# Attention one: where the products for the row maxima stand among the scores

## What is computed

```python
h = h + _L0_attn_ref(_layernorm(h, axis=-1), Wqkv, bqkv, Wr, br)

def _L0_attn_ref(x, Wqkv, bqkv, Wr, br):          # b 8, c 1024, h 16, he 16
    xh = x.reshape(b, c, h, he).transpose(0, 2, 1, 3)
    q, k, v = jnp.split(jnp.einsum('bhce,ef->bhcf', xh, Wqkv) + bqkv, 3, axis=-1)
    att = jnp.einsum('bhqe,bhke->bhqk', q, k) / jnp.sqrt(jnp.float32(he))
    mask = jnp.tril(jnp.ones((c, c), dtype=att.dtype), k=-1)
    att = jax.nn.softmax(att * mask, axis=-1)
    out = jnp.einsum('bhqk,bhke->bhqe', att, v)
    return out.transpose(0, 2, 1, 3).reshape(b, c, d) @ Wr + br
```

## Time and profile before

| | |
|---|---|
| median of three runs | 2999.05 us (2997.51 to 3005.18) |
| profiled execution | 3005.22 us, its span 3002.8 us |
| first attention | about the first 1500 us of the span, 14 loop iterations of two windows in it |
| mean granted TensorE clock | 0.928 of full speed |

### The profile page before, as it was taken

How to read it: one execution, slowest core, us unless ns; L and a number is a source line. 1 busy time by engine, 2 the same in 40 slices (tenths; PEclk the granted TensorE clock), 3 DMA queues, 4 the chain that set the end, 5 groups by cost and what they waited for, 6 DMA issues and landing times. The chain is left out here.

```text
span 3002.8 us, 58475 instructions
## 1 busy us (share of the span) xinstructions
PE 2581.3 (86%) x15254; PEld 1510.3 (50%) x15318; DVE 2118.6 (71%) x5668; ACT 1523.5 (51%) x3246; POOL 1640.4 (55%) x2564
## 2 busy tenths in 40 slices
PE   1778988888988888888868999898998979999999
PEld 0323433333333333343345666666666647666666
DVE  2657766777766767676567999898888965556554
ACT  1345555555555655555513655555555634444444
POOL 3664343333334333334245877777776757777675
PEclk7679999999999999999969999999999979999999
DMA  3353343344343344334230000000000000000000
GB/s 56 89 116 62 52 63 54 52 70 69 51 63 56 53 59 70 58 54 63 36 137 1 1 1 1 1 1 1 1 1 1 1 3 16 16 14 16 16 16 18
DMA packets 81300, 113.27 MB, mean 38 GB/s; under 512 B 25100, under 2 KB 37144, under 8 KB 80536
## 3 DMA queue, kind: packets, MB, share of 16 engines
q1 hardware_dynamic: 76360, 101.44, 19.8%
q0 software_dynamic: 3072, 8.39, 1.0%
q10 hardware_dynamic: 1744, 2.16, 0.2%
HBM read 18.98 MB, written 8.39 MB: 9 GB/s over the span
## 5 line engine op out<-in xcount | busy, mean ns | idle before, releaser
L554 ACT ACTIVATE probs<-scoresT 128x512 f32<-128x512 f32 x1152 | 639.7, 604 | 632.4 <-PE scoresT L697 622.9
L643 DVE TENSOR_REDUCE cand<-ring 128x4 f32<-128x512 f32 x1152 | 724.1, 680 | 219.6 <-PE ring L753 167.3
L476 POOL TENSOR_SCALAR_AFFINE_SELECT probs<-probs 128x256 f32<-128x256 f32 x512 | 204.9, 414 | 468.5 <-ACT probs L554 462.4
L697 PE MATMUL scoresT<-stage 98*128 98x512 bf16 (+3 forms) x1536 | 410.3, 344 | 22.2 <-ACT probs L554 16.6
L753 PE MATMUL ring<-Km,Qm 64*128 64x512 bf16 (+2 forms) x1792 | 253.0, 321 | 160.5 <-DVE cand L643 130.5
L717 PE MATMUL pv<-probs,Vg 128*32 128x512 f32 (+3 forms) x3072 | 325.2, 545 | 28.3 <-POOL probs L476 25.9
L753 PEld LDWEIGHTS ring<-Km,Qm 64*128 64x128 bf16 x1792 | 83.5, 95 | 375.6 <-DVE cand L643 239.5
L1180 PE MATMUL mm<-w_W,hT 128*128 128x256 f32 x1024 | 259.1, 399 | 8.7 <-ACT z L1268 2.8
L1200 PE MATMUL mm<-w_W,x2T 128*128 128x512 f32 x512 | 242.4, 596 | 0.3 <-DVE x L1419 0.2
L697 PEld LDWEIGHTS scoresT<-stage 98*128 98x128 bf16 x1536 | 114.5, 99 | 234.4 <-issue 139.1
L1261 ACT ACTIVATE hT<-mmT,w_be,w_g 128x128 f32<-128x128 f32 x512 | 185.5, 469 | 90.7 <-PE mmT L1191 90.7
(11 more groups left out here) (254 smaller groups left out, 5280.9 us busy)
## 6 DMA issues: line engine op xcount, KB each, us to landing
stage<-parts SPq DMA_DIRECT2D x256, 96.0 KB, 2.8
stage<-parts SPq DMA_DIRECT2D x256, 64.0 KB, 2.8
Qm<-parts SPq DMA_DIRECT2D x128, 128.0 KB, 2.6
Km<-parts SPq DMA_DIRECT2D x128, 128.0 KB, 2.7
stage<-parts SPq DMA_DIRECT2D x256, 32.0 KB, 2.4
out<-result SPq DMA_DIRECT2D x64, 128.0 KB, 1.7
stage<-ct SPq DMA_DIRECT2D x128, 4.0 KB
w_W<-in_W SPq DMA_DIRECT2D x4, 512.0 KB
```

The costliest lines, as they stand in the source:

```text
L476: nc.gpsimd.affine_select(out=d, in_=d, compare_op=ALU.is_gt, fill=0.0, base=0, pattern=[[0, 2], [1, P]], channel_multiplier=-1).then_inc( ...
L554: nc.scalar.activation(probs[:, buffer(slot), :], scoresT[slot % SCORE_BANKS][:], ACT.Exp, scale=SOFT).then_inc(exp_ok, 1)
L643: ins = nc.vector.tensor_reduce(c, src[:].rearrange("p (t a b) -> p t a b", t=c.shape[1], b=P), AX.X, ALU.max)
L697: ins = nc.tensor.matmul(scoresT[slot % SCORE_BANKS][:, at:at + hi - lo], Ks[0:ROWS, gi, hh, P * kt:P * kt + P], Qs[0:ROWS, gi, hh, lo:hi] ...
```

## The change

The units of the maxima are put two at a time (four banks, the whole ring) at nine positions `MAX_AT`, the same in both windows, instead of one at a time at 18. Bursts 0 to 3 move from 9, 12, 20, 28 to 11, 15, 22, 30, so that with bursts 4 and 5 (at 0 and 3, unmoved) six of the nine groups have a burst at their position. `PV_HALF`, the copy of the first half of `pv`, moves from 14 to 17, behind burst 1. In the prologue without scores (`ALONE`) the units stand one position apart.

```diff
-BURST_AT = {0: 9, 1: 12, 2: 20, 3: 28}
+BURST_AT = {0: 11, 1: 15, 2: 22, 3: 30}
+
+MAX_AT = (0, 3, 7, 11, 15, 18, 22, 26, 30)
...
-    0: {... "MX": 2, "MX_END": 32, "MX_CURVE": 1.0, "PV_HALF": 14},
-    1: {... "MX": 1, "MX_END": 32, "MX_CURVE": 1.0, "PV_HALF": 14},
+    0: {... "PV_HALF": 17},
+    1: {... "PV_HALF": 17},
...
-         "WR": 14, "VG": 14, "LOAD": 14, "MX": 15, "MX_END": 35, "MX_CURVE": 1.0}
+         "WR": 14, "VG": 14, "LOAD": 14, "MX": 15}
...
-        lo, hi = pos_of["MX"], pos_of["MX_END"]
         for n, u in enumerate(uses):
-            at(int(lo + (hi - lo) * (n / len(uses)) ** pos_of["MX_CURVE"]), *u)
+            at(MAX_AT[n // 2] if scores else pos_of["MX"] + n, *u)
```

More of the change, by code:

```diff
@@ L137 @@
 AT = {
-    0: {"LN_STATS": 1, "LN_NORM": 3, "XT": 7, "PV_COPY": 4, "EQ": 6, "TMP": 0, "PT": 5, "OT": 24, "WR": 25, "RSUM": 5, "SUF": 12, "QK": (11, 13, 18, 20), "MID_LAG": 2, "V": 21, "VG": 5, "LOAD": 0, "MX": 2, "MX_END": 32, "MX_CURVE": 1.0, "PV_HALF": 14},
-    1: {"PV_COPY": 4, "EQ": 6, "TMP": 0, "PT": 5, "WR": 1, "V": 8, "VG": 6, "LOAD": 0, "MX": 1, "MX_END": 32, "MX_CURVE": 1.0, "PV_HALF": 14},
+    0: {"LN_STATS": 1, "LN_NORM": 3, "XT": 7, "PV_COPY": 4, "EQ": 6, "TMP": 0, "PT": 5, "OT": 24, "WR": 25, "RSUM": 5, "SUF": 12, "QK": (11, 13, 18, 20), "MID_LAG": 2, "V": 21, "VG": 5, "LOAD": 0, "PV_HALF": 17},
+    1: {"PV_COPY": 4, "EQ": 6, "TMP": 0, "PT": 5, "WR": 1, "V": 8, "VG": 6, "LOAD": 0, "PV_HALF": 17},
     "V_IN": 0, "WR_IN": 1,
```

## The result

The changed kernel takes 3148.55 us (median of four runs, 3146.12 to 3156.26); the kernel before took 3000.76 beside it. The ratio is 1.0496, interval 1.0473 to 1.0519: slower by 148 us. The forecast was 3110 us, slower by 111.

What follows compares the result with a forecast made beforehand. TensorE leads, busy 1115.70 of 1300 us in attention, and waits mostly on VectorE's reductions. Terms -4.3 + 0.3 + 3.8 + 4.25 + 2.8 + 0.6 = +7.45 us per iteration, times 15, gave 3110 us; range 2947 to 3160.

Steps and rivals of the forecast that it cites:

- Step 1: TensorE, both windows: 43 fewer changes of form at 0.10 us, -4.3 us per iteration, less 0.3 before the long wait.
- Step 2: Window 0: four reductions ahead of LN_STATS delay statistics, rstd and LN_NORM; TensorE waits before PT: +3.8 us per iteration.
- Step 3: Both windows: groups fill the ring, next users wait for VectorE's or ScalarE's reads: +4.25 us per iteration net.
- Step 4: Both windows, behind groups: the fourth score in a row costs about 0.4 us: +2.8 us per iteration.
- Step 4's other half: End of the windows: burst 3 moved from 28 to 30 leaves two scores elsewhere: +0.6 us per iteration.
- The factor of 15: Each iteration's change counts about 15 times, 14 in the loop and one in the halves written out: +112 us.
- rival C: Longer waits put one more burst per iteration at the lower clock, 19 us in all: 3150 to 3180; chance 0.1.
- Rival A: Pauses decide, the full ring's new waits don't come: -3.45 us per iteration, 2947 us; chance 0.15.
- Rival B: Layer norm's 3.8 eats the pauses' 4.0, new waits replace old: within 9 us of 2999; chance 0.08.

Runs made afterwards that it cites:

- groups-alone run: Changed kernel with bursts back at 9, 12, 20, 28 and PV_HALF at 14, the groups of four banks kept: 3147.14 us, ratio 1.0486.
- Short exponentials: From the second half on, ScalarE's exponential takes 128 of 512 columns per score bank: changed kernel 3062.77 us, kernel before 3000.15 us.
- the bursts alone: Kernel before with bursts at 11, 15, 22, 30 and PV_HALF at 17, units spread as before: 2999.22 us, ratio 0.9987.
- two versions with `rstd` early: Spread units, later bursts, GpSimd's rstd at position 0 instead of 3: 2952.5 us with LN_NORM at 3, 2983.41 us with it at 4.
- run with rstd early: Spread units with the later bursts, GpSimd's rstd at position 0 instead of 3, LN_NORM at 3: 2952.5 us, ratio 0.9827.

## Why the prediction was right, and where its size was off

**Step 1, the pauses**: right in kind. Counted over TensorE's products in 13 iterations of either trace, changes of form fell from 91.9 to 48.9 per iteration, by the forecast 43, and units within a group stand 0.22 apart. That makes 4.3 us; but TensorE's busy time, which holds the pauses, fell by 0.34. No run isolates the price; the groups-alone run saw seven pauses as 0.38 us of busy time, less than the 0.7 of the forecast.

**Step 2, the layer norm behind four reductions**: shown. In the iteration above TensorE goes on 16.36 us after the start of burst 4, and the working gave 839.75 - 823.39 = 16.36; that the digits agree is luck, since the iterations run from 15.9 to 16.7. The means differ by 3.7 us, for a forecast of 3.8. Moving the statistics alone won 46 of the 57 us that this step was put at. The rest fits `rstd`'s place on GpSimd, which the step left out of account: with the statistics moved it still begins 0.7 us later than before, and TensorE goes on 0.8 later.

**Step 3, the full ring**: right. `QK` 2.85 us per iteration against 1.0 + 1.75, `PT`'s banks 1.06 against 1.2, `CT` behind the group 0.66 per window against 0.6. With VectorE's other 34.3 and 3.0 us (2.45 and 0.21 per iteration) these new waits make 7.9, against 7.5. Moving `QK` won 36 us.

**Step 4, the scores in a row**: the place was right, the size isn't settled. It counted seven new fourth scores of 0.4 us, 2.8 per iteration or 42 us. The list shows 107 such waits in 14 iterations, 7.6 per iteration, where the kernel before has about three; so some 4.6 are new, which at 0.42 each make 1.9. Short exponentials took 83 us more from the changed kernel than from the one before, but that is not the price of these waits alone: the exponentials also stand before `QK`'s reads (39.9 us of waits fell to 24.6), and up to 2.15 of the 4.94 us per iteration that the changed kernel gained are the clock's.

**Step 4's other half, the ends of the windows** (0.6): its reason, burst 3's later place, is not what the runs show, since the bursts alone cost nothing. A wait that the sum had left out stands there instead: `CT` at the end waits 0.99 us for GpSimd instead of 0.45, in either window, also in the groups-alone run; which makes 1.1 per iteration.

**The sum**: the sign and the places were right and the size too small, 7.45 for a measured 10.36 us per iteration. By the traces the 10.36 are +10.70 of idle time and -0.34 of busy time. The forecast had waits of 11.45 (3.8 + 4.25 + 2.8 + 0.6). The recorded ones make 10.7, and a wait costs more than its record: a fourth score is recorded with 0.26 and comes 1.08 - 0.66 = 0.42 late. Some ten waits more per iteration (24 against 14) at 0.16 (0.42 less 0.26) make 1.6, an estimate; so the waits come to about 12.3, 0.9 over the forecast. The largest part that is missing is the clock, for which the sum had no term: 13.3 instead of 10.1 us of work at the lower level, which costs up to 1.6. About 0.5 are left, by which the pauses gave back less than the forecast 4.0; this is a remainder and was not measured. The factor of 15 was high as well: 148 us are 14.3 times 10.36, which hid some 5 us of the shortfall.

The clock stood in rival C with a chance of 0.1, as one burst more at the lower level, 19 us in all; the result lies just under C's 3150 to 3180 (whose middle is 3165, not the 3160 that closes the range). Up to 1.6 us per iteration is up to 23 us in all, so C's price was near, but its place was not. In window 0, with its longer wait, hardly more work ran at the lower level: 8.0 us before and 8.2 after. In window 1 it rose from 2.2 to 5.0: most of burst 4 ran there at the lower level in each of the 14 iterations, and in seven a second stretch at it came 24 to 28 us after that burst's start. The timeline is also not quite the same in every iteration, as the prediction took it: before, burst 4 of window 1 ran at the lower level in most iterations and not in all. Why the clock fell at these places, no run isolates.

**Rival A** needed the reductions to keep up. With reductions of 0.42 instead of 0.68 us in both kernels the changed one stays 117 us behind, so that alone would not have been enough: the order, ScalarE's reads and the exponentials cost as well. **Rival B** falls with the result. The Trainium skill ("TensorEngine Tiling (Array Packing)", PSUM Bottleneck) says that copying out of PSUM may become the bottleneck once tiling has made the products faster. The halved reductions agree (134 and 107 us); ScalarE's reads are a part of it (36 us for `QK`).

## What to carry to other kernels

Before packing products of one form together, follow the buffers that they fill: a group as large as the ring turns every reader's delay into a wait of the next user, whatever engine reads it. Where engines work through one list of events, an instruction moved ahead of another engine's short chain (here four reductions ahead of the statistics) delays all of that chain; look there first, since moving one small instruction (`rstd`) gained 47 us, where the pauses had been put at 60 and the groups that were to save them lost 148. And sum busy time and idle time apart, and the busy time by clock level: an order with less idle time can be the slower one when more of its work runs at the lower level.

## What the runs showed of the hardware that was not expected

The granted clock doesn't follow the amount of idle time alone. In the two versions with `rstd` early, 10.79 us idle per iteration left a clock of 0.95 over 13 iterations and 9.04 left 0.91, and the iteration was 85.42 and 87.68 us long. Nor does the longest wait decide: it was 4.60 us where the clock stayed higher and under 2 us where it fell lower. What decides, these runs don't show.

`LN_NORM` runs at two speeds, by what GpSimd does beside it. Two iterations of the run with rstd early, burst 4 on TensorE and `LN_NORM` on VectorE:

```profile
881.80 3.15 PE L719 MATMUL pv<-probs,Vg 128*32 128x512 f32 x16 [0.30 <-POOL probs L478]
...
966.22 1.71 PE L719 MATMUL pv<-probs,Vg 128*32 128x512 f32 x16 [0.25 <-POOL probs L478]
```

```profile
887.38 2.24 DVE L622 TENSOR_SCALAR xn<-h,mv,rstd 128x128 f32 x8
...
971.61 3.64 DVE L622 TENSOR_SCALAR xn<-h,mv,rstd 128x128 f32 x8 [1.28 <-POOL rstd L486]
```

and GpSimd's suffix sums in the same two, which a copy precedes, and before it in the first a mask:

```profile
889.63 0.41 POOL L478 TENSOR_SCALAR_AFFINE_SELECT probs<-probs 128x256 f32<-128x256 f32 x1 [1.63 <-ACT probs L556]
889.99 0.29 POOL L501 COPY Rsum<-Vh 128x128 f32<-128x128 f32 x1
890.36 3.36 POOL L503 TENSOR_TENSOR Rsum<-Rsum,Vh 128x128 f32<-128x128 f32 x6
...
972.75 0.29 POOL L501 COPY Rsum<-Vh 128x128 f32<-128x128 f32 x1
973.13 3.11 POOL L503 TENSOR_TENSOR Rsum<-Rsum,Vh 128x128 f32<-128x128 f32 x6
```

Where the sums begin behind `LN_NORM`, its eight instructions take 2.24 us; where the copy begins 1.1 us into it, 3.64. The first is so in 5 of the 14 iterations, and they are those whose burst 4 ran at the lower clock level (2.7 to 3.2 us instead of 1.71): there a mask that GpSimd makes before the copy waits for its exponential until 889.63; in the others it need not wait. Window 0 takes 47.4 to 47.7 us in these five and 49.8 in the others, but window 1 behind it takes 37.05 instead of 35.8. About 1.1 us per iteration is left, 5 us in all: half of the 11 by which the gain exceeded the forecast; the other half is not explained. Before, the sums began with `LN_NORM` in all iterations (3.87 us). GpSimd's own time is no longer beside `LN_NORM` (3.11) than beside VectorE's later work (3.36). The Trainium skill ("SBUF — State Buffer", Who interferes with whom) has VectorE and GpSimd share a pair of ports under an exclusive lock. The rows agree that VectorE suffers: beside the sums one instruction of `LN_NORM` takes 0.61 us instead of 0.33, and one ends for each of GpSimd's, which keep their 0.45. Whether VectorE stands still for the whole of each, the rows can't tell. So a further version would begin the sums behind `LN_NORM` in every iteration; it wasn't run.
